# A graph kernel's edge loop on one core: y made in two halves, the accT addition moved between hs and msg

## The reference, cut to what matters

```python
f = (e @ fc_w.T).reshape(-1, 4, 128)            # e: 100000 x 128, fc_w: 512 x 128
w = attn[rel]                                   # 100 relations, 4 heads x 128
feat = sum over heads of leaky_relu(w * f, 0.2)
msg = h[src] + feat
x = layernorm(x + segment_sum(msg, dst))        # first layer
...                                             # second layer: attention over the same edges, layernorm
```

## Time and profile before

| | us |
|---|---|
| median of 3 runs | 2626.28 |
| lowest, highest | 2620.51, 2626.96 |
| span of the profiled execution (its time as a run isn't shown) | 2618.1 |
| VectorE busy in it | 2255.1 |
| TensorE busy in it | 2159.8 |
| GpSimd busy in it | 1919.3 |
| ScalarE busy in it | 1740.7 |

### The profile page before, as it was taken

One profiled execution on the slowest core, in us unless ns is written; L12 is line 12 of the kernel. 1 busy time (PEld: TensorE's weight loads), 2 busy tenths in 40 slices (PEclk: granted clock), 3 DMA queues, 4 the chain that ended last, 5 costly groups with the idle time before them and its releaser, 6 DMA issues.

```text
span 2618.1 us, 44445 instructions
## 1 busy us (share of the span) xinstructions
PE 2159.8 (82%) x11261; PEld 1538.3 (59%) x11261; DVE 2255.1 (86%) x5754; ACT 1740.7 (66%) x4973; POOL 1919.3 (73%) x1845
## 2 busy tenths in 40 slices
PE   6999999999999999999999846665666666666664
PEld 3566666666666666666666535565656565556554
DVE  9999999999999999999999976666666666677887
ACT  5888888888888888888888644444444444444446
POOL 2487777777777777777777647777777777777773
PEclk8999999999999999999999877777677767777776
DMA  4233333333333333333333233333333333333343
GB/s 133 78 100 104 104 104 103 106 103 102 103 103 105 104 105 105 103 103 102 103 104 104 65 95 81 80 80 80 81 81 80 81 81 82 79 81 79 80 80 80
DMA packets 156600, 244.04 MB, mean 93 GB/s; under 512 B 40836, under 2 KB 84398, under 8 KB 156226
## 3 DMA queue, kind: packets, MB, share of 16 engines
q1 hardware_dynamic: 97730, 132.55, 17.9%
q0 software_dynamic: 58624, 108.72, 17.5%
HBM read 231.99 MB, written 9.12 MB: 92 GB/s over the span
## 4 chain that ended last, share of the span: by engine, by line
DVE 36%; issue 25%; POOL 18%; PE 7%; DMA 6%; DVEq 5%; ACT 1%; POOLq 0%; SPq 0%; ACTq 0%
POOL room L583 17%; DVE y L1231 17%; DVE hs L1239 9%; DMA room<-h_rows,y 5%; DVEq L1211 4%; DVE room L1255 4%; PE FP L986 3%; DVE accT L1215 2%; PE FP L1007 2%; PE AP L1007 1%; DVE z L1224 1%; DMA room<-h_rows,idx 1%; DVE joh L1205 1%; POOL room L591 1%; DVE room L1247 1%
## 5 line engine op out<-in xcount | busy, mean ns | idle before, releaser
L539 POOL DMA_INDIRECT room<-in_x,pk x784 | 920.7, 1174 | 262.5 <-issue 251.0
L583 POOL DMA_INDIRECT room<-h_rows,y x756 | 714.7, 945 | 235.2 <-issue 216.0
L896 PE MATMUL FP<-fc_sb,room 128*128 128x512 f32 x1568 | 832.3, 612 | 2.2 <-issue 2.2
L905 PE MATMUL WP<-at_p,rel_oh 100*128 100x512 f32 x1568 | 803.5, 594 | 0.0
L986 PE MATMUL FP<-ident,room 128*128 128x128 f32 x1664 | 342.7, 370 | 385.9 <-DMA room<-h_rows,y 351.7
L659 ACT ACTIVATE w_sb<-WP 128x512 f32<-128x512 f32 x784 | 464.1, 592 | 225.0 <-PE WP L905 219.7
L986 PEld LDWEIGHTS FP<-ident,room 128*128 128x128 f32 x1664 | 291.0, 263 | 433.3 <-DMA room<-h_rows,y 387.1
L757 ACT ACTIVATE accT<-accT,neg_big 128x512 f32<-128x512 bf16 x208 | 150.0, 722 | 559.6 <-DVE accT L1377 559.6
L905 PEld LDWEIGHTS WP<-at_p,rel_oh 100*128 100x128 f32 x1568 | 297.8, 190 | 376.5 <-issue 376.5
L1224 DVE TENSOR_TENSOR z<-FP,w_sb 128x1024 f32<-128x1024 f32 x392 | 478.6, 1221 | 1.6 <-ACT w_sb L659 1.0
L1231 DVE SCALAR_TENSOR_TENSOR y<-z 128x2048 f32<-128x2048 f32 x196 | 452.4, 2308 | 0.0
(11 more groups left out here) (246 smaller groups left out, 3181.6 us busy)
## 6 DMA issues: line engine op xcount, KB each, us to landing
room<-in_e SPq DMA_DIRECT2D x196, 256.0 KB, 2.7
rel_sb<-in_rel_g SPq DMA_DIRECT2D x196, 200.0 KB
z<-sorted_sources SPq DMA_DIRECT2D x208, 128.0 KB, 3.0
room<-in_x,pk POOLq DMA_INDIRECT x784
room<-h_rows,y POOLq DMA_INDIRECT x756
sorted_edges<-runs,spot_i POOLq DMA_INDIRECT x196, 2.0
accT<-in_x_t SPq DMA_DIRECT2D x1, 3125.0 KB, 11.2
h_rows<-arena SPq DMA_DIRECT2D x13, 227.5 KB, 2.8
```

The costliest lines, as they stand in the source:

```text
L539: pool.indirect_dma_start(xg[:, k, u, 0:P], None, x[:, :], bass.IndirectOffsetOnAxis(ap=pk[:, g, u:u + 1], axis=0)).then_inc(xg_in[k], 16)
L583: pool.indirect_dma_start(hg[k][:, u, :], None, h_dram[:, :], bass.IndirectOffsetOnAxis(ap=sd[:, g * TG + u:g * TG + u + 1], axis=0)).then ...
L896: mm = pe.matmul(FP[u // 2][:, u % 2, :], e_sb[:, k, u, :], fc_sb[:, :], start=True, stop=True)
L905: mm = pe.matmul(WP[u % 2][:, :], rel_oh[:, k % 2, u * P:(u + 1) * P], at_p[:, j, :], start=(j == 0), stop=(j == 1))
```

## The change

`slope` over both halves becomes `slope_pair` for one half. The first half is made between msg and the second z, the other at the group's end. `accumulate` moves from behind the second z to between hs and msg. The semaphore `y_done` now counts halves.

```diff
                 if not (lead and k == 0):
-                    dve.wait_ge(y_done, g)
+                    dve.wait_ge(y_done, 2 * g - 1 + h)
                 v.tensor_tensor(z[:, h, :, :], FP[h][:, :, :], w_sb[:, h, :, :], ALU.mult).then_inc(z_done, 1)
 
-            def slope(g, k, lead):
-
-                dve.wait_ge(z_done, 2 * g + 2)
+            def slope_pair(g, k, lead, h):
+
+                dve.wait_ge(z_done, 2 * g + h + 1)
                 if not (lead and k == 0):
                     dve.wait_ge(hs_done, g)
-                v.scalar_tensor_tensor(y[:, :, :, :], z[:, :, :, :], SLOPE0, z[:, :, :, :], ALU.mult,
+                v.scalar_tensor_tensor(y[:, h, :, :], z[:, h, :, :], SLOPE0, z[:, h, :, :], ALU.mult,
                                        ALU.max).then_inc(y_done, 1)
 
             def halve(g, k, lead):
 
-                dve.wait_ge(y_done, g + 1)
+                dve.wait_ge(y_done, 2 * g + 2)
...
                 weigh_pair(g, k, lead, 0)
                 if prev:
                     halve(*prev)
-                    finish(*prev)
-                weigh_pair(g, k, lead, 1)
                 if not (lead and k < 2):
                     accumulate(g - 2, (k - 2) % SLOTS, lead)
                 if prev:
+                    finish(*prev)
+                slope_pair(g, k, lead, 0)
+                weigh_pair(g, k, lead, 1)
+                if prev:
                     add_x(*prev)
-                slope(g, k, lead)
+                slope_pair(g, k, lead, 1)
```

## The result

| us | before | the change |
|---|---|---|
| median | 2624.86 (4 runs) | 2731.38 (4 runs) |
| lowest, highest | 2620.51, 2626.96 | 2725.54, 2742.81 |
| span of the profiled execution | 2618.1 | 2723.8 |

The ratio is 1.0414, with a 95% interval of 1.0389 to 1.0439. The forecast was 2622; the measured time is within 26 us of the first rival's price (2757). The ratios leave out two of the eight executions of experiment 3, at 2935 and 4075 us, which nothing here explains.

The account below looks back on a forecast made before the run. VectorE was taken to bound the edge loop, with GpSimd just keeping pace. Its terms gave -0.03 us per group, plus 0.01 for disturbance of y: -0.02 x 196 = -4 us, from 2626.3 to 2622 us, range 2612 to 2775.

Parts of the forecast that it names:

- What bounds the kernel: In the edge loop VectorE sets the pace at 7.17 us per group, and GpSimd, held by it, keeps pace exactly.
- (a): On VectorE, y is cut into two halves of 1.22 to 1.24 us each: +0.06 to +0.10 us per group.
- (b): On VectorE, the addition to accT fills the dependent gap between hs and msg: -0.11 us per group.
- (c): add_x goes behind the first half of y, making TensorE's aggregate 1.0 us later: cost nothing, with 0.35 us as cover.
- The slit: Between two VectorE operations that hold GpSimd, it can slip in until some 0.07 us behind the first one's end.
- In the slit: GpSimd asks at 7.29 us, is let in ahead of joh, fits five operations per period and keeps pace; chance 0.43.
- Missed: joh holds GpSimd to 0.28 us, then possibly hs to 2.58: four operations per period where five are needed.
- Rival 1: GpSimd sets the pace and add_x waits for its gather: +0.67 us per group, +131 us, 2757 us; chance 0.34.
- z waiting for ScalarE's copy: Sign that the prediction is wrong altogether: VectorE's z waits for ScalarE's copy of TensorE's products, forecast to have 0.35 us left.
- Rival 2: GpSimd costs VectorE nothing and the halves overlap cleanly: -0.05 us per group, -10 us, 2616 us; chance 0.16.
- Rival 3: TensorE or ScalarE late by more than the 0.35 us of cover, or no overlap on VectorE: 2646 us; chance 0.07.
- the rule of the Trainium skill: VectorE's next operation starts only when the pipe is empty: the split costs +0.13 us per group, +25 us; chance 0.03.

Follow-up runs that it names:

- experiment 3: The change with the first half of y ahead of msg instead of behind it; 2614.58 us, ratio 0.9969 to the kernel before.
- experiment 1: The change with accumulate back behind the second z, so only y is split; 2628.25 us, ratio 1.0026 to the kernel before.
- experiment 4: The change with three gathers per group instead of four, the fourth tile's product taking the first's rows; 2608.22 us, ratio 0.9947 to the kernel before.
- experiment 5: The kernel before with three gathers per group instead of four, the fourth tile's product taking the first's rows; 2626.94 us, ratio 1.0009.
- Experiment 8: The change with eight buffers for the scatter's rows instead of four; 2659.92 us, ratio 1.0149 to the kernel before.
- experiment 6: The change with a VectorE memset of 162 unused columns behind the second z, ahead of add_x; 2753.70 us, ratio 1.0492 to the kernel before.
- experiment 7: The change with a memset of 162 unused columns behind add_x, ahead of the second half of y; 2622.77 us, ratio 1.0007 to the kernel before.
- experiment 2: The kernel before with only accumulate moved between hs and msg, y left whole; 2855.66 us, ratio 1.0882.
- experiment 10: The change reordered: hs ahead of the first z, accumulate between the first half of y and the second z; 2608.72 us, ratio 0.9939 to the kernel before.

## Why the prediction was wrong, by its steps

**What bounds the kernel**: right. GpSimd stood at its limit in the kernel before, without a gap by which it could be seen, and this was the right question to ask.

**(a) the halves**: forecast 1.23 each, measured 1.218. **(b) the filled gap**: hs to addition 1.14 and addition to msg 0.13, as forecast. **(c)** add_x later by one half: as forecast, at no cost by itself; experiment 1 shows it. The sum on VectorE alone was forecast at 7.12 to 7.16 per period and is 7.07 in the groups that nobody delays: the halves added 0.05 (2.27 from the first steps of both against 2.22), the gap gave 0.11, and three other steps are 0.01 to 0.02 shorter than in the kernel before. Experiments 4 and 5 give 16 us of gain where the forecast had 4.

**The slit**: the step that failed. "In the slit" was taken as the likelier case, with a request at 7.29 and a slit open until 7.29. Two terms behind it were mis-sized, by 0.02 each. From add_x's end to the second y's end I had 1.15; the rows give 810.62 - 809.49 = 1.13. From a release to the next request I had 1.22; the held gather ended 0.81 behind the release, the gap is 0.31 and the request, by the estimate, comes 0.12 behind the start: 1.24. The request falls at 1.24, the slit closes at 1.20. "Missed" was the truth, with its four per period. The error behind this is one of judgement: two sides so close together should have had even chances instead of 0.43 against 0.34, with a loss of 131 us on one side and a gain of 4 on the other.

**Rival 1**: right in mechanism, that GpSimd sets the pace, and near in period (7.84 forecast, 7.67 measured) and time (2757 and 2731). That the size came so near was in part luck: it was an even split between full pace and 8.53, a period built on a wait for the gather's landing, and this wait didn't occur. It gave 0.67 us per group over the kernel before; 0.50 came, or 0.60 over VectorE's own 7.07. The place of the wait was wrong. add_x never waited for its gather inside the loop (behind it, the last one did, for 2.74 us). The late scatter stopped ScalarE first, and through the copies the first z. I had looked at the four slots of the gathers and not at the four buffers of the scatter, on the same queue. Experiment 8 shows what this overlooked buffer is worth: 2731 against 2660. The prediction named "z waiting for ScalarE's copy" as a sign that it was wrong altogether; the sign appeared, but behind the late scatter, and not behind the later add_x of (c).

**The loop's end**: the lag has to be paid there too. The last joh starts 97.1 us later than before (1577.93 against 1480.86), the first bn_stats behind the loop 104.6 later (1603.0 against 1498.4): GpSimd's last four scatters, from 1588.29 to 1598.36, all ran behind VectorE's last y, which ended at 1585.80.

**Rival 2** was near on VectorE's own work (-0.05 per group forecast, -0.10 measured) and wrong on GpSimd. **Rival 3** is refuted by experiment 1, which is as late and 103 us faster. So is the size that I gave to the rule of the Trainium skill (page "VectorE: DVE Perf Modes", section "The DRAIN you can't avoid"), +0.13 per group for the split: it cost 0.04 (7.21 against 7.17), and a memset of 0.19 us costs 0.11 (experiments 6 and 7), so the overlap stays. The section itself lets a next operation that isn't held start earlier, and that is what the rows show.

## What to carry to other kernels

An engine with a little idle time by its sums can be exactly at its limit, when its operations are held by another's and its rhythm is locked to that one; look at what its long operations end with. Making the pacing engine faster may then throw the other out of step: with y whole, 0.11 us less work per group on VectorE cost some 230 us (experiment 2); with y in halves, 0.11 us more of useless work won 109 back (experiment 7). Whoever reorders a queue of VectorE beside a queue of indirect DMAs should count, for one period, the moments at which GpSimd is let in, and check every buffer that hangs on that queue.

## What the runs showed of the hardware

- A GpSimd indirect DMA that asks while VectorE runs an operation with two SBUF inputs is held to that operation's end and ends 0.77 to 0.87 later. Between two back-to-back operations of this kind it is let in if it starts some 0.05 or more ahead of the end of the first (experiments 5 and 7). Whether it does can decide over 1 to 2 us.
- The hold works in both directions: add_x takes 0.62 instead of 0.54 when a gather has just been let in (experiment 10, 54 groups). I had expected 0.03 to 0.04, and on y. The Trainium skill, page "SBUF — State Buffer", section "Who interferes with whom", says of the two-port modes that whoever issues first has the port pair for the whole instruction. For GpSimd's DMA and a two-input operation these runs show less: a gather of 0.95 us holds VectorE for 0.08.
- Behind a memset the next operation takes hold earlier than behind an accumulate: add_x is 0.49 long instead of 0.55, and a gather that starts 0.10 ahead of its start is refused (experiment 6), where behind an accumulate one that starts 0.01 to 0.06 ahead is let in, 177 times (experiment 1).
